# Edge pass of a graph-attention and feed-forward kernel: target scores of four chunks in fourteen by VectorE and ScalarE, not by TensorE

## The reference

```python
ft = jnp.einsum('nhd,od->nho', hv, W)          # hv: layernorm(x) as (n, 12, 64)
a1 = jnp.sum(ft * attn_l, axis=-1)
a2 = jnp.sum(ft * attn_r, axis=-1)
e = leaky_relu(a1[src] + a2[dst], 0.2)
w = exp(e - segment_max(e, dst)[dst])
alpha = w / maximum(segment_sum(w, dst)[dst], 1e-16)
agg = segment_sum(alpha[:, :, None] * ft[src], dst)
x = x + relu(agg + einsum('nhd,od->nho', hv, W_res))
x = x + concat([experts(layernorm(x)[:6]), gelu(layernorm(x)[6:] @ W1 + b1) @ W2 + b2])
```

## Time and profile before

| | before |
|---|---|
| median of three runs | 2741.15 us (2739.52 to 2741.22) |
| the profiled execution: time, span | 2742.36 us, 2740.6 us |
| mean granted TensorE clock | 0.984 |
| busy in the span: PE, DVE, ACT, POOL | 2638.7, 2397.8, 2378.1, 2137.9 us |
| edge pass with all stages filled | from about 70 to 950 us |

### The profile page before, as it was taken

One profiled execution on the slowest core, in us unless ns is written; L12 is line 12 of the kernel. 1 busy time (PEld: TensorE's weight loads), 2 busy tenths in 40 slices (PEclk: granted clock), 3 DMA queues, 4 the chain that ended last, 5 costly groups with the idle time before them and its releaser, 6 DMA issues. The chain is left out here.

```text
span 2740.6 us, 69176 instructions
## 1 busy us (share of the span) xinstructions
PE 2638.7 (96%) x21454; PEld 2393.8 (87%) x21454; DVE 2397.8 (87%) x4888; ACT 2378.1 (87%) x4745; POOL 2137.9 (78%) x2029
## 2 busy tenths in 40 slices
PE   5999999999999974999999999999999999999998
PEld 4888888888888853899999999999999999999996
DVE  4688888888888774999999999999999999999994
ACT  4988888888888844999999999999999999999982
POOL 6777777777777614888888888888888888888881
PEclk9999999999999995999999999999999999999998
DMA  8787777777877637899999999999999999988973
GB/s 312 213 258 253 255 253 255 253 253 253 252 254 253 203 120 254 311 346 345 334 332 331 320 328 327 316 324 318 310 325 318 313 319 313 313 314 312 313 251 126
DMA packets 256712, 777.96 MB, mean 284 GB/s; under 512 B 79719, under 2 KB 87699, under 8 KB 256371
## 3 DMA queue, kind: packets, MB, share of 16 engines
q1 hardware_dynamic: 183980, 563.28, 58.3%
q0 software_dynamic: 69312, 210.37, 24.9%
q10 hardware_dynamic: 3176, 1.29, 0.2%
HBM read 638.90 MB, written 236.69 MB: 319 GB/s over the span
## 5 line engine op out<-in xcount | busy, mean ns | idle before, releaser
L942 PE MATMUL ps<-wr_bd,arena 128*128 128x128 f32 x4704 | 597.8, 277 | 25.2 <-DVE arena L1290 22.6
L942 PEld LDWEIGHTS ps<-wr_bd,arena 128*128 128x128 f32 x4704 | 565.9, 194 | 28.5 <-issue 25.3
L649 POOL DMA_INDIRECT arena<-agg_scratch,nrow x392 | 440.0, 1122 | 79.8 <-issue 67.8
L627 POOL TENSOR_SCALAR arena<-csr_neg,mv,r_n 128x768 f32<-128x768 f32 x392 | 390.1, 995 | 50.9 <-PE ps L796 37.3
L1285 DVE SCALAR_TENSOR_TENSOR ps<-ps,r_n,arena 128x768 f32<-128x768 f32 x392 | 399.0, 1018 | 26.1 <-PE ps L942 17.1
L741 ACT ACTIVATE t_hi<-ps 128x768 fp32r<-128x768 f32 x392 | 315.7, 805 | 85.5 <-PE ps L796 85.4
L1290 DVE SCALAR_TENSOR_TENSOR arena<-ps,arena 128x768 f32<-128x768 f32 x392 | 375.5, 958 | 13.4
L639 POOL TENSOR_SCALAR arena<-arena,nm_n,r_n 128x768 f32<-128x768 f32 x392 | 384.9, 982 | 0.8 <-PE ps L796 0.4
L729 ACT ACTIVATE arena<-arena,mv 128x768 f32<-128x768 f32 x392 | 368.0, 939 | 12.7
L1297 DVE TENSOR_TENSOR t_lo<-ps,t_hi 128x768 fp32r<-128x768 f32 x392 | 373.5, 953 | 2.8 <-ACT t_hi L741 2.7
L750 ACT ACTIVATE arena<-arena,s_st 128x768 f32<-128x768 f32 x392 | 363.4, 927 | 14.2 <-DVE arena L1290 14.2
(11 more groups left out here) (208 smaller groups left out, 6160.9 us busy)
## 6 DMA issues: line engine op xcount, KB each, us to landing
arena<-in_x SPq DMA_DIRECT2D x196, 768.0 KB
arena<-in_x_cols SPq DMA_DIRECT2D x392, 384.0 KB, 5.1
out<-arena SPq DMA_DIRECT2D x195, 768.0 KB, 5.8
agg_scratch<-agg_ring SPq DMA_DIRECT2D x196, 384.0 KB, 3.0
dst_all<-in_dst_rows SPq DMA_DIRECT2D x28, 256.0 KB, 4.0
arena<-agg_scratch,nrow POOLq DMA_INDIRECT x392
arena<-in_x,e_slot POOLq DMA_INDIRECT x364, 4.6
dst_all<-in_dst_rows SPq DMA_DIRECT2D x28, 192.0 KB
```

Source lines behind the costliest of these rows:

```text
L627: pool.tensor_scalar(g_ring[:, g, :].rearrange("p (c f) -> p c f", f=P), csr_neg[:, None, :].to_broadcast([P, NC, P]), mv1[:, w, 2 * (v % ...
L649: pool.indirect_dma_start(g_ring[:, g, :], None, agg_d, bass.IndirectOffsetOnAxis(nrow[:, v, 3:4], 0), bounds_check=EP - 1, oob_is_err=Fal ...
L942: last = nc.tensor.matmul(pair(1)[:, i * P:(i + 1) * P], xt_ring[:, g, i * P:(i + 1) * P], wr_bd[:], start=True, stop=True)
```

## The change

In four of each fourteen chunks (`OFF_PE = (2, 5, 9, 12)`, "off chunks"; modulo 7 these are 2 and 5, twice) the target scores don't come from TensorE. `v2_row`, the score weights as a row of 768, the same on all partitions, is made once at the start. For an off chunk:
- TensorE transposes only the source rows (6 instead of 12) and leaves out L850 and L870;
- ScalarE copies 512 and 256 columns instead of three times 512, then makes a copy of the target rows times -1/768 with an accumulated sum, which is the mean (`s_mean`); the copy lands in `both_t` and is overwritten. L692 falls away;
- VectorE makes `(target row + (-mean)) * v2_row` into `both_t`, after L1104 and ahead of L1116 in the step of the transposes (positions 4 and 0), and in the next step (positions 5 and 1) sums it per head into `a2_all`, ahead of L1104. The copy L1095 falls away one step later (positions 6 and 2).

Three semaphores of the softmax become one with three counts (`s_seg`), and VectorE's waits for the copy of the scores count the chunks that still have one.

```diff
@@ -57,6 +57,8 @@
 HM = HEADS + 1
+OFF_PE = (2, 5, 9, 12)
+N_ON = BODY - len(OFF_PE)
@@ -94,6 +96,16 @@
 
+def on_pe(b, i):
+
+    return N_ON * (b + i // BODY) + sum(v not in OFF_PE for v in range(i % BODY))
+
+
+def off_pe(b, i):
+
+    return len(OFF_PE) * (b + i // BODY) + sum(v in OFF_PE for v in range(i % BODY))
+
+
...
@@ -676,10 +689,22 @@
                         at_least(act, s_ft, ct - 1)
-                        at_least(act, s_sc, ct - 1)
-                        for k in range(NBLK):
-                            act.wait_ge(s_tr, NBLK * ct + k + 1)
-                            nc.scalar.activation(both_t[:, v, k * BLK:(k + 1) * BLK], ps[:, k, :], ACT.Copy).then_inc(s_etr, 1)
+                        at_least(act, s_sc, on_pe(b, i - L_TR - 1))
+                        if (i - L_TR - 2) % BODY in OFF_PE:
+                            at_least(act, s_a2c, ct - 1)
+                        if (i - L_TR) % BODY in OFF_PE:
+                            vd = (i - L_TR) % BODY
+                            act.wait_ge(s_tr, NBLK * ct + 1)
+                            nc.scalar.activation(both_t[:, v, 0:BLK], ps[:, 0, :], ACT.Copy).then_inc(s_etr, 1)
+                            act.wait_ge(s_tr, NBLK * ct + NBLK)
+                            nc.scalar.activation(both_t[:, v, BLK:D], ps[:, 1, 0:D - BLK], ACT.Copy).then_inc(s_etr, NBLK - 1)
+                            act.wait_ge(d_gd[vd % G], 16 * (2 * b + (i - L_TR) // G + 1))
+                            nc.scalar.activation(both_t[:, v, D:2 * D], xd_ring[:, vd, :], ACT.Copy, scale=-1.0 / D,
+                                                 accum_out=a2_all[:, vd // G, vd % G, HEADS:HM]).then_inc(s_mean, 1)
+                        else:
+                            for k in range(NBLK):
+                                act.wait_ge(s_tr, NBLK * ct + k + 1)
+                                nc.scalar.activation(both_t[:, v, k * BLK:(k + 1) * BLK], ps[:, k, :], ACT.Copy).then_inc(s_etr, 1)
@@ -687,9 +712,10 @@
                             .then_inc(s_eft, 1)
-                        act.wait_ge(s_sc, cf + 1)
-                        at_least(act, s_sct, cf)
-                        nc.scalar.activation(sc_row, sc_ps, ACT.Copy).then_inc(s_esc, 1)
+                        if vf not in OFF_PE:
+                            act.wait_ge(s_sc, on_pe(b, i - L_FT) + 1)
+                            at_least(act, s_sct, on_pe(b, i - L_FT))
+                            nc.scalar.activation(sc_row, sc_ps, ACT.Copy).then_inc(s_esc, 1)
@@ -802,17 +828,17 @@
                         v = (i - L_TR) % BODY
-                        for k in range(NBLK):
+                        for k in range(2 if v in OFF_PE else NBLK):
                             if k == 0:
                                 pe.wait_ge(s_norm, ct + 1)
-                            if k == 1:
+                            if k == 1 and v not in OFF_PE:
                                 pe.wait_ge(d_gd[v % G], 16 * (2 * b + (i - L_TR) // G + 1))
                             at_least(pe, s_etr, NBLK * (ct - 1) + k + 1)
-                            for m in range(4 * k, 4 * k + 4):
+                            for m in range(4 * k, min(4 * k + 4, NC if v in OFF_PE else 2 * NC)):
                                 src = xs_ring if m < NC else xd_ring
                                 last = nc.tensor.transpose(ps[:, k, m % 4 * P:(m % 4 + 1) * P],
                                                            src[:, v, m % NC * P:(m % NC + 1) * P], ident[:])
-                            last.then_inc(s_tr, 1)
+                            last.then_inc(s_tr, NBLK - 1 if k == 1 and v in OFF_PE else 1)
...
@@ -850,7 +876,7 @@
                         last.then_inc(s_sc, 1)
-                    if exists(c - L_SQD, EC):
+                    if exists(c - L_SQD, EC) and (i - L_SQD) % BODY not in OFF_PE:
@@ -865,8 +891,14 @@
                                          ft_ring[:, v, 4:NC, 0:P], start=True, stop=True).then_inc(s_sum, 1)
-                    if exists(cf, EC):
-                        pe.wait_ge(s_esc, cf + 1)
+                    if isinstance(b, int) and c == L_TR:
+                        pe.wait_ge(s_v, 6)
+                        nc.tensor.matmul(sum_ps[:, 0:512], ones[:], v2_row[:, 0:512], start=True, stop=True)
+                        nc.tensor.matmul(sum_ps[:, 512:D], ones[:], v2_row[:, 512:D], start=True, stop=True).then_inc(s_pre, 1)
+                    if exists(cf, EC) and (i - L_FT) % BODY not in OFF_PE:
+                        pe.wait_ge(s_esc, on_pe(b, i - L_FT) + 1)
+                        if isinstance(cf, int) and cf == 0:
+                            pe.wait_ge(s_v, 7)
@@ -1091,8 +1123,27 @@
                         w, j = v // G, v % G
-                        dve.wait_ge(s_sct, c2 + 1)
-                        V.tensor_copy(a2_all[:, w, j, :], a2_ps).then_inc(s_a2c, 1)
+                        if v not in OFF_PE:
+                            dve.wait_ge(s_sct, on_pe(b, i - L_SQD) + 1)
+                            V.tensor_copy(a2_all[:, w, j, :], a2_ps).then_inc(s_a2c, 1)
+
+                    if isinstance(b, int) and c == 8:
+                        link_up(V.tensor_tensor(tmp_f[:, 0:NC], v26[:, :, HEADS], v26[:, :, HEADS + 1], ALU.add))
+                        V.tensor_tensor(v2_row.rearrange("p (n f) -> p n f", f=P), ident[:, None, :].to_broadcast([P, NC, P]),
+                                        tmp_f[:, 0:NC][:, :, None].to_broadcast([P, NC, P]), ALU.mult).then_inc(s_v, 1)
+                    if isinstance(b, int) and c == L_FT:
+                        dve.wait_ge(s_pre, 4)
+                        V.tensor_copy(v2_row, sum_ps).then_inc(s_v, 1)
+                        dve.wait_ge(s_v, 7)
+
+                    cr = c - L_FT
+                    if exists(cr, EC) and (i - L_FT) % BODY in OFF_PE:
+                        v = (i - L_FT) % BODY
+                        w, j = v // G, v % G
+                        dve.wait_ge(s_prod, off_pe(b, i - L_FT) + 1)
+                        V.tensor_reduce(a2_all[:, w, j, 0:HEADS],
+                                        both_t[:, v % 2, D:2 * D].rearrange("p (h d) -> p h d", d=DH), axis=AX.X, op=ALU.add)\
+                            .then_inc(s_a2c, 1)
@@ -1105,6 +1156,14 @@
                             .then_inc(s_eo, 1)
+
+                    cp = c - L_TR
+                    if exists(cp, EC) and (i - L_TR) % BODY in OFF_PE:
+                        v = (i - L_TR) % BODY
+                        w, j = v // G, v % G
+                        dve.wait_ge(s_mean, off_pe(b, i - L_TR) + 1)
+                        V.scalar_tensor_tensor(both_t[:, v % 2, D:2 * D], xd_ring[:, v, :], a2_all[:, w, j, HEADS:HM], v2_row,
+                                               ALU.add, ALU.mult).then_inc(s_prod, 1)
@@ -1162,14 +1221,14 @@
                         if exists(cf, EC):
-                            dve.wait_ge(s_esc, cf + 1)
+                            at_least(dve, s_esc, on_pe(b, i - L_FT + 1))
                         V.tensor_copy(e_row[:], row_ps[:, 0:P])
                         V.tensor_copy(same_r[:, 0:P], row_ps[:, P:2 * P]).then_inc(s_same, 1)
                     if (i - 21) % G == 0 and exists(ga, NG):
                         w = (i - 21) // G % 2
                         dve.wait_ge(s_wst, ga + 1)
                         if exists(cf, EC):
-                            dve.wait_ge(s_esc, cf + 1)
+                            at_least(dve, s_esc, on_pe(b, i - L_FT + 1))
...
```

More of the change, by code:

```diff
@@ L197, in gnn_ffn_kernel @@
         sel3 = part(36164, HM, rows=NCT * CT)
+        v2_row = part(36180, D)
         ones = sb("ones", [P, P])
@@ L337, in gnn_ffn_kernel @@
         s_a2c = sem("s_a2c")
+        s_mean = sem("s_mean")
+        s_prod = sem("s_prod")
         s_mask = sem("s_mask")
@@ L341, in gnn_ffn_kernel @@
         s_same = sem("s_same")
[L342 to L344 removed]
+        s_seg = sem("s_seg")
         s_z = sem("s_z")
```

17 lines of the change are left out of this document (7 added, 10 removed).

## The result

The changed kernel takes **2810.88 us** (median of 4 runs, 2808.99 to 2813.86), the one before 2741.18 beside it: a ratio of 1.0254, with a 95% interval of 1.0238 to 1.027. The profiled execution has a span of 2807.6 us (before 2740.6) and a mean granted clock of 0.978. The change moves lines: L1104 is now L1155, L1116 L1175, L1088 (ve_d) L1120, L1095 L1128, L864 L890, L866 L892, L813 L839; new are the product L1165, the sum per head L1144 and the mean L702.

A forecast was written before the change was run, and what follows sets the result against it. TensorE was taken to set the pace, 34.55 us per group of seven; after the change a path through VectorE, 24.8 + 2.45 + 10.06 = 37.3, adds 2.76 over 24.6 groups: 68 us, with 1 for the weights' row 2810 (2790 to 2830).

The forecast's parts named there:

- product and sum per head, busy: VectorE's two new 768-column operations per off chunk: 0.95 us each, about one element a cycle.
- wait for the mean, position 4: VectorE's product, ahead of L1116, waits there for ScalarE's mean: 1.3 us.
- wait for the mean, position 0: VectorE's product waits there for the mean, ScalarE being held by position 6's exponential: 0.5 us.
- L1155 position 4 to position 1: VectorE's path between these L1104 (now L1155): 19.28 old work, 3.80 new, less 0.08, plus two waits: 24.8 us.
- to TensorE's next step: From position 1's L1104: itself 1.01, a signal 0.05, TensorE's sum 1.39, no selection product: 2.45 us.
- positions 2 and 3: TensorE's two steps run freely, then features, square, ve_d and L1104 follow as before: 10.06 us.
- The first piece: VectorE's path from L1104 of position 4 to L1104 of position 1: 24.8 us a group.
- The second piece: From L1104 of position 1 to TensorE's next step, with a signal of 0.05: 2.45 us a group.
- rival 4: TensorE's clock drops after its new waits; one half-level stretch per group, 2.6 us, gives 2874; 6%.
- The fill and the rest: Outside the steady steps: fill and drain savings left at nothing, the weights' row at the start 1 us.
- rival 1: VectorE absorbs the work, its waits disappearing: 34.4 us a group, or 33.6, 23 us less in all, 2718; 14%.
- Rival 2: VectorE's product does not wait for the mean: 1.8 us off, 0.96 a group longer, 2766; 13%.

The follow-up runs named there:

- e1_busy: The changed kernel with 18 more small products on TensorE at position 1, ahead of the sum, nobody reading them; 2792.55 us, 1.0183 of the kernel before.
- e2_order: The changed kernel with VectorE's sum per head moved behind L1155 and L1175 and the product to its step's end; 2736.86 us, 0.9981 of the kernel before.
- e7_place_order: The changed kernel with OFF_PE = (1, 6, 8, 13), sum per head behind L1155 and L1175, product at the step's end; 2695.08 us, 0.9828 of the kernel before.
- e6c_shortmean: The changed kernel with ScalarE's mean over one column, ahead of the copies, VectorE's code unchanged; 2773.04 us, 1.0115 of the kernel before.
- e10_waits: The changed kernel with twelve already satisfied waits added in VectorE's loop body; 2851.69 us, 1.0409 of the kernel before.

## Why the prediction was right, and where its terms were off

The mechanism was that forecast: VectorE's chain takes TensorE's saving and as much again. The time was met to within 1 us, which the terms were not: two of them were off in opposite directions, and the small ones at either end took the rest. That they cancel so closely is luck; what was right is the path, the places of the waits and the size of each piece to within 0.7 us in a group without the clock's drop.

| term, us a group | predicted | measured |
|---|---|---|
| product and sum per head, busy | 0.95, 0.95 | 1.02, 0.94 |
| wait for the mean, position 4 | 1.3 | 1.19 |
| wait for the mean, position 0 | 0.5 | 0 and 0.60 in turn |
| L1155 position 4 to position 1 | 24.8 | 24.18 and 24.11 |
| to TensorE's next step | 2.45 | 2.52; 3.83 with the slow sum |
| positions 2 and 3 | 10.06 | 10.03; 10.40 with the slow transposes |
| group | 37.3 | 36.73 and 38.34 |

The pieces are read from the rows above: 652.44 - 628.26 = 24.18, 654.96 - 652.44 = 2.52, 664.99 - 654.96 = 10.03; in the group ahead of it 614.03 - 589.92 = 24.11, 617.86 - 614.03 = 3.83, 628.26 - 617.86 = 10.40.

*The first piece was 0.6 to 0.7 too long.* The prices were right as busy times, but on the path an instruction costs what lies between its start and that of the next, and their ends overlap: 631.41 - 630.47 = 0.94 for the product and 635.47 - 634.61 = 0.86 for the sum, 0.2 a group less than the 3.80 of the prediction. The old instructions of the four steps took less as well. Without the new ones and the waits, the four steps from 628.26 on take 4.22, 5.18, 5.17 and 4.82 (the first is 635.47 - 628.26 = 7.21 less 0.94, 0.86 and 1.19), where the prediction has 4.48, 5.31, 4.50 and 4.91, the copy of position 6 taken off. Less the 0.68 of the loop's turn in the third, that is some 0.5 shorter: starts that were up to 0.2 further apart before, beyond the waits in brackets, have moved together. That VectorE, running behind, finds more of its small waits over is a likely reason and not shown. The waits were 0.1 too long at position 4 and either 0.5 too long or 0.1 too short at 0; and where the wait at 0 is missing, the loop's turn stands in its place, which no term of the sum had.

*The second piece was 0.1 too short.* From the end of L1155 to the sum 653.59 - 652.44 - 1.00 = 0.15 us pass, and not 0.05.

*One reading was loose.* ScalarE's copies at position 4 do not start right behind the square: the normalization of source rows, 0.92 from start to start, stands between. The start that the sum used, 624.06, is the measured one, so nothing in it moves.

*The clock was not 1.00.* A granted clock below 1 in the steady stretch stood among the signs of being wrong, and it was 0.98: rival 4 came true in part. It was priced as all or nothing, at 2.6 us in each group and with 6%; the group with the drop takes 38.34 - 36.73 = 1.61 more, 0.8 in the mean. The path 0.57 shorter and these 0.8 longer make 37.53 instead of 37.3, 2.97 more than the 34.56 before instead of 2.76: 71 us over the 24 groups counted, where I had 68 over 24.6. The fill and the rest, which I put at nothing and at +1, came out at -4, so the spans differ by 67 where I had 69. e1_busy gives the clock's part as 18 us by itself. The other 51 us are the path that was forecast, and e2_order takes all of the loss away by moving instructions alone. Without the drop the forecast's path would have ended at e1_busy's 2793, near the lower end of its own range.

*The rivals.* VectorE did not absorb it: every wait foreseen at position 4 was there (ve_d 1.29, product 1.19). But rival 1's condition, TensorE and ScalarE ahead of VectorE, can be had by moving the work (e7_place_order), and then gives more than the 23 us I gave it: 2742.85 - 2695.08 = 48, as VectorE's work is 31.4 us a group there and not the 33.6 to 34.4 of that rival. Rival 2 is refuted by 19.7 us of waits of the product between 300 and 800. The rule on `tensor_reduce` of the Trainium skill (VectorE: DVE Perf Modes, Rules for kernel authors) calls it the slowest operation. The trace has it at 944 ns, under the product's 1018 and L1175's 952, so here the measurement does not agree. It is close to the 0.957 us estimated from the formula on the same page of the Trainium skill. The sum cost about as much as its neighbours; with the same sum in another place (e2_order) the loss is gone.

*What stays open.* I have not shown why the clock's drop keeps to every second group. The wait ahead of it is 0.35 longer there, 2.67 against 2.32, yet e6c_shortmean drops after 1.97 in one group and not after 2.30 in another; so the length of this one wait alone does not decide it. Nor is it known whether VectorE's stop at the loop's turn comes with the length of the body (none at 293 instructions, a stop at 298) or with where the body lies behind the code ahead of it.

## What to carry to other kernels

Moving work from a full engine to one with idle time pays only where that idle time is: two engines that wait for each other in every step form a chain, and what counts is where in the chain the new instructions stand. Here the same operations cost 70 us in one place and, with other chunks taken off and another order on VectorE, gained 48. Before moving work, follow the longest path round one period, put the instruction that waits last in its step, behind everything the other engine is waiting for, and take off only as many chunks as fill the second engine.

## What was unexpected of the hardware

- In the changed kernel waits of TensorE of 2.67 us were followed by 1.7 us lost at half clock (2.04 and 1.06 instead of 1.10 and 0.59 for the sum), and waits of 2.32 in the groups between were not. In e6c_shortmean waits of 1.97 and of 2.30 were followed by it in some groups and not in others, in those shown only from the transposes on (2.77 instead of 1.47). Filling the wait with products that nobody reads brought 18 us.
- With a loop body of 298 or 299 VectorE instructions the engine stood still for 4.4 and 3.7 us at every turn in the mean, where with one of 293 it waited 0.2: 176 packets in the instruction queue against 121, and 41 us in e10_waits for twelve waits that were over long before.
